# States of the retention layers from token-major keys, values projected once and spread by ScalarE

## The chip, the cores and the metric

One core of one Trainium2 chip runs the whole program. The metric is the device time of one execution in microseconds (us); the median of the runs counts. Engines: PE is TensorE, DVE VectorE, ACT ScalarE, POOL GpSimd, SP SyncE.

## What is computed

Four blocks run one after the other on 2048 tokens of width 128: a selective scan, a soft decision tree, four retention layers and a choice among eight experts, each with norms and residuals. The change touches the retention layers. Cut to that:

```python
Q, K, V = (x @ Wq), (x @ Wk), (x @ Wv)           # 8 heads of 16
Q, K = _rotate(Q, cos, sin), _rotate(K, cos, -sin)
att = jnp.einsum('bnhd,bmhd->bhnm', Q, K) * Dm    # decay gamma^(n-m), n >= m
Y = jnp.einsum('bhnm,bmhd->bnhd', att, V)
Y = normalise(Y) * gn_s + gn_b                     # over the 16 of a head
Yr = (swish(x @ Wg) * Y) @ Wo + X                  # x = layer_norm(X)
X = gelu(layer_norm(Yr) @ W1) @ W2 + Yr
```

## The kernel before

Everything lies in SBUF, in fp32. The tokens are four groups of 512 (two sequences of 256, four tiles of 128). A sequence is cut into chunks of 64. Attention inside a chunk is worked out directly (**scores**, masked by DVE); what earlier chunks contribute goes through a state, keys transposed times values for a chunk (**states**), of which DVE keeps the blocks of one head (its mask), and which **mix** multiplies with the queries. Decay is folded into the tables with which keys and queries are turned.

A layer is a list of steps. SCHEDULE gives each a time in units of one group's turn; the steps of the four groups are sorted by it into one order, LAYER, and every engine goes through this order and issues its part of each step. OPENING is the same list for the first layer, sorted together with the steps of the tree; ENDING that of the last layer, with the steps of the experts (d_turn, logits, oh_turn, hidden, expert). So a turn of the steady part holds each step once, for different groups. An engine waits where a semaphore isn't there yet, and what stands behind waits too.

The steps of a group that the text speaks of, in the order of its way: stats1, norm1 (DVE, with the rstd by POOL, L521 and L523), **turn1** (PE transposes, ACT copies to Ht, L799), **rotate** (PE L1428, keys and queries token-major; DVE L1085 multiplies by cosines into Tc and by sines into Ts), **gate** (PE L1447, ACT's Tanh L814, DVE L1090), **spread** (POOL L628 adds Tc and Ts for keys, then for queries; PE transposes L1435; ACT makes masked copies Ka and Qp), **keys** (PE transposes the masked copies back, L1453; ACT copies to Kt, L833), **values** (PE L1443; ACT L808 writes Va, in which even and odd heads lie on different partitions), **scores** (PE L1464, DVE L1100), **states** (PE L1473, DVE L1110), **mix** (PE L1485 and L1491), **gather** (ACT L836), **heads** and **var** (PE L1499, DVE, POOL's power L636, unit L1131), **out_turn**, **scale** (DVE L1135), **out** (PE L1239, DVE L1138), stats2, norm2 (DVE L919), **ffn_turn**, **ffn_up** (PE L1517, gelu on ACT L853), **ffn_down** (PE L1239, DVE's addition L1146).

PSUM has eight banks of 512 columns. FILLS says which bank a step of PE fills and which event frees it; claim makes PE wait for the event of the bank's last use:

```python
for event, of, at_group, nth in held.get(b, ()):
    pe.wait_ge(*event.at(of, at_group, nth))
held[b] = [(reader, layer, g, k)]
```

Banks 2 and 3 hold scores and, in the ending, hidden; experts use 6 and 7; oh_turn uses 5, d_turn and logits use 1, in both versions.

## Time and profile before

| | |
|---|---|
| median of 3 runs | 774.08 us (773.95 to 774.34) |
| profiled execution | 775.45 us, of which the span from first to last instruction 773.7 |
| PE, DVE, POOL, ACT busy | 649.6, 616.8, 441.6, 426.0 us |
| mean granted clock of PE | 0.95 |

Busy times are sums over the span; the stretches of it have different limits. A PE matmul in fp32 is two records in the trace, a transpose one; their ends are modelled and overlap the next one's start.

### The profile page before, as it was taken

The page shows a single profiled execution, that of the slowest core. Times are in us where ns is not written, and L with a number is a line of the kernel's source. Part 1 is how long each engine was busy: PE and PEld are TensorE (multiplying, and loading weights), DVE is VectorE, ACT ScalarE, POOL GpSimd, SP SyncE. Part 2 cuts the span into 40 slices and gives each one's busy share as a digit, 9 for nine tenths or more (in the row PEclk, how much of TensorE's full clock was granted, in tenths as well). Part 3 has the DMA queues.
Part 4 walks back from the last instruction along what each step waited for, and adds up shares of the span by engine and source line. Part 5 has one row for each costly group of instructions (what it writes and reads, how often), then busy time and mean ns, then how long its engine had stood idle before and what let it go on. Part 6 is the DMA issues. An engine that isn't in the chain of part 4 may idle for free. (4 is left out here: it accounts for less than half of the span.)

```text
span 773.7 us, 13393 instructions
## 1 busy us (share of the span) xinstructions
PE 649.6 (84%) x4919; PEld 449.8 (58%) x4928; DVE 616.8 (80%) x1519; ACT 426.0 (55%) x745; POOL 441.6 (57%) x411
## 2 busy tenths in 40 slices
PE   3997798898988853547889999999999999889994
PEld 1435444444444342545767777777777777657673
DVE  6479798998989777474778888888888888778886
ACT  1896785886767405445545555555555555354551
POOL 6113588786877947564565555556666666452212
PEclk9997799999999996796999999999999999999998
DMA  9003033233233300000000000000000000000000
GB/s 321 13 5 54 28 98 92 82 99 92 77 89 86 75 2 0 0 1 0 2 2 22 2 6 16 21 2 5 15 1 22 3 18 1 2 0 1 1 27 29
DMA packets 17297, 27.37 MB, mean 35 GB/s; under 512 B 2320, under 2 KB 7056, under 8 KB 16976
## 3 DMA queue, kind: packets, MB, share of 16 engines
q1 hardware_dynamic: 17232, 26.51, 12.1%
q8 instruction: 40, 0.66, 0.3%
q14 instruction: 25, 0.20, 0.1%
HBM read 25.32 MB, written 1.18 MB: 34 GB/s over the span
## 5 line engine op out<-in xcount | busy, mean ns | idle before, releaser
L584 POOL TENSOR_TENSOR arena<-arena 128x1024 f32<-128x1024 f32 x64 | 150.1, 2363 | 52.3 <-PE psum L1340 26.8
L1010 DVE TENSOR_TENSOR_SCAN arena<-arena,psum 128x1024 f32<-128x1024 f32 x64 | 141.8, 2269 | 3.3 <-issue 2.0
L1340 PE MATMUL psum<-arena,Cs 128*128 128x512 f32 x256 | 121.9, 599 | 1.2 <-POOL arena L584 1.2
L721 ACT ACTIVATE arena<-arena 128x510 f32<-128x510 f32 x128 | 84.9, 711 | 51.8 <-DVE arena L1010 49.8
L521 POOL TENSOR_TENSOR ve<-mv,eps 128x4 f32<-128x4 f32 x52 | 15.9, 305 | 166.4 <-DVE mv L908 166.4
L636 POOL TENSOR_TENSOR arena<-arena,mhalf 128x32 f32<-128x32 f32 x16 | 86.8, 5428 | 4.5 <-DVE arena L1126 4.5
L1232 PE MATMUL psum<-Cs,arena 128*128 128x128 f32 x240 | 40.2, 292 | 43.0 <-ACT arena L764 25.9
L1340 PEld LDWEIGHTS psum<-arena,Cs 128*128 128x128 f32 x256 | 45.2, 191 | 46.4 <-issue 35.0
L1232 PEld LDWEIGHTS psum<-Cs,arena 128*128 128x128 f32 x240 | 27.8, 147 | 57.9 <-ACT arena L764 27.1
L628 POOL TENSOR_TENSOR arena<-arena 128x256 f32<-128x256 f32 x64 | 57.8, 935 | 2.4 <-DVE arena L1085 2.4
L1239 PE MATMUL psum<-Wl,arena 128*128 128x128 f32 x384 | 51.3, 285 | 5.9 <-DVE arena L1135 5.4
L523 POOL TENSOR_TENSOR rs<-ve,mhalf 128x4 f32<-128x4 f32 x52 | 53.4, 1027 | 4.1
L1323 PE MATMUL psum<-Cs,arena 128*128 128x128 f32 x256 | 35.2, 284 | 23.9 <-ACT arena L743 20.7
L1323 PEld LDWEIGHTS psum<-Cs,arena 128*128 128x128 f32 x256 | 30.2, 146 | 42.2 <-issue 37.6
L743 ACT ACTIVATE arena<-arena 128x256 f32<-128x256 f32 x128 | 54.2, 495 | 0.0
L1239 PEld LDWEIGHTS psum<-Wl,arena 128*128 128x128 f32 x384 | 46.9, 197 | 9.4 <-DVE arena L1135 8.8
L1239 PEld LDWEIGHTS psum<-Wd,arena 128*128 128x128 f32 (+1 forms) x320 | 39.5, 191 | 16.1 <-issue 7.0
L904 DVE BATCH_NORM_STATS2 st<-arena 128x6 f32<-128x128 f32 x208 | 45.2, 280 | 3.9 <-ACT arena L764 2.6
L919 DVE TENSOR_SCALAR arena<-arena,mv,rs 128x128 f32<-128x128 f32 x160 | 44.6, 343 | 3.7 <-POOL rs L523 3.7
L1100 DVE TENSOR_TENSOR arena<-psum,Cs 128x512 f32<-128x512 f32 x64 | 41.0, 683 | 6.5 <-PE psum L1464 6.5
L1239 PE MATMUL psum<-Wd,arena 128*128 128x128 f32 (+2 forms) x320 | 41.8, 276 | 2.8 <-DVE arena L1209 1.4
L1215 DVE SCALAR_TENSOR_TENSOR arena<-psum,arena 128x128 f32<-128x128 f32 x128 | 35.9, 344 | 8.9 <-PE psum L1239 7.5
(175 smaller groups left out, 1396.6 us busy)
## 6 DMA issues: line engine op xcount, KB each, us to landing
arena<-c_rows_by_state SPq DMA_DIRECT2D x32, 512.0 KB, 4.7
Wl<-wl SPq DMA_DIRECT2D x4, 384.0 KB, 3.1
Wd<-wd SPq DMA_DIRECT2D x1, 1100.0 KB, 10.8
X<-x SPq DMA_DIRECT2D x4, 256.0 KB, 6.9
Sel<-sel SPq DMA_DIRECT2D x1, 1024.0 KB, 8.9
Wl<-wl SPq DMA_DIRECT2D x4, 256.0 KB, 2.7
out<-X SPq DMA_DIRECT2D x4, 256.0 KB, 2.3
Cs<-const SPq DMA_DIRECT2D x1, 614.0 KB, 9.6
```

Of the source, the lines that this page charges most:

```text
L523: pool.tensor_tensor(rs[:, g * GT:(g + 1) * GT], ve[:, g * GT:(g + 1) * GT], mhalf[:, 0:GT], ALU.pow).then_inc(rstd_ready, 1)
L584: pool.tensor_tensor(Hc[:, h], Hs[:, r, h], Crows[:, r], ALU.mult).then_inc(hc_ready, 1)
L628: ins = pool.tensor_tensor(to[:, :, :, e], to[:, :, :, e], other[:, :, :, 1 - e], ALU.add)
L636: pool.tensor_tensor(gst[:, cols], gst[:, cols], mhalf[:], ALU.pow).then_inc(rstd_ready, 1)
L721: ins = act.activation(Da[:, h, group(e)].rearrange(seq, s=S)[:, :, 1:], Dt[:, h, group(g)].rearrange(seq, s=S)[:, :, 1:], ACT.Exp, scale= ...
L743: ins = act.activation(Wslot[n % 2][:, part, k, :], Flip[g % 2][:, k * 256:(k + 1) * 256], ACT.Identity, scale=Bt_rows[:, column:column + 1])
L904: own.put(dve.bn_stats(st3[:, t, :], src3[:, t, :]))
L1010: dve.tensor_tensor_scan(Hs[:, turn % 2, h], Da[:, h], rows_of(turn, h), 0.0, ALU.mult, ALU.add).then_inc(scanned, 1)
L1232: ins = pe.transpose(dst[:, tile(k)], src3[:, g * GT + k, :], ident)
L1239: ins = pe.matmul(dst[:, k * width:(k + 1) * width], r[:, tile(k)], w, start=i == 0, stop=i == len(rows) - 1)
L1323: ins = pe.transpose(rows[:, tile(e * GT + k)], Wslot[slot % 2][:, e, k, tile(h)], ident)
L1340: ins = pe.matmul(bank[h], ident, Hc[:, h, group(e)], start=False, stop=False, skip_group_check=True)
```

## The change

Keys are no longer transposed back. States multiplies the token-major turned keys in Tc, 64 tokens of a tile at a time, with plain values Vt in the same tokens; even chunks lie in rows 0 to 63, odd ones in rows 64 to 127, and the two kinds fill two banks (even chunks of both sequences in bank 5, 512 columns, odd ones in bank 7, 256), so that DVE's two masks have these widths. Values is four matmuls of 128 columns, token-major; ACT copies them whole to Vt and then in four quarters to Va, between partitions where needed. Several steps move to other banks. The times of SCHEDULE change, by which gate comes ahead of mix on PE and ahead of gather on ACT, in the opening rx_stats of groups 2 and 3 ahead of the states masks of groups 0 and 1 on DVE, and in the ending x_stats of group 0 ahead of the masks of group 3, and stats2 of group 3 ahead of group 0's last expert sum; else the order on DVE and POOL is the old one.

```diff
-    (1.142, "spread", 1), (1.309, "keys", 0), (1.296, "scores", 0), (1.515, "values", 0), (1.012, "gate", 0),
-    (1.516, "scores", 1), (1.562, "states", 0), (1.957, "mix", 0), (2.010, "gather", 0), (2.068, "heads", 0),
+    (1.138, "spread", 1), (1.299, "scores", 0), (1.511, "values", 0), (0.964, "gate", 0), (1.514, "scores", 1),
+    (1.737, "states", 0), (1.966, "mix", 0), (2.039, "gather", 0), (2.077, "heads", 0), (2.291, "square", 0),
...
-        Kt = take(4 * (SEQ_CHUNKS - 1) * P).rearrange("p (b n) -> p b n", b=4)
+        Vt = take(2 * GT * P).rearrange("p (t n) -> p t n", n=P)
...
-            "rotate": ((4, rotated, 2), (1, rotated, 4)), "spread": ((5, k_spread, 1), (4, q_spread, 1)),
-            "values": ((1, v_ready, 1),), "gate": ((1, sg_ready, 1),),
-            "keys": ((7, k_tokens, 1), (5, k_tokens, 2)), "states": ((5, states, 1), (7, states, 2)),
-            "mix": ((6, yt_rows, 1),), "out": ((4, r_mid, 1),), "ffn_up": ((4, gelu_ready, 1), (7, gelu_ready, 2)), "ffn_down": ((7, r_newer, 1),)}
+            "rotate": ((4, rotated, 2), (1, rotated, 4)), "spread": ((5, k_spread, 1), (1, q_spread, 1)),
+            "values": ((4, v_ready, 1),), "gate": ((7, sg_ready, 1),),
+            "states": ((5, states, 1), (7, states, 2)),
+            "mix": ((6, yt_rows, 1),), "out": ((5, r_mid, 1),), "ffn_up": ((1, gelu_ready, 1), (4, gelu_ready, 2)), "ffn_down": ((4, r_newer, 1),)}
...
                         act.wait_ge(*v_done.at(layer, g))
                         act.wait_ge(*added.at(layer, g - 2))
-                        for a in range(PARITY):
-                            half_rows = slice(CHUNK * a, CHUNK * a + CHUNK)
-                            dst = Va[half_rows, chunks, :].rearrange("p c (j w) -> p (c j) w", j=PAIR)[:, :, DH * a:DH * a + DH]
-                            ins = act.copy(dst, bank[FILLS[what][0][0]][half_rows, :].rearrange("p (c i) -> p c i", i=DH))
-                            if a == 0:
-                                own.put(ins)
+                        tiles = slice(g % 2 * GT, (g % 2 + 1) * GT)
+                        rows = bank[FILLS[what][0][0]]
+                        own.put(act.copy(Vt[:, tiles, :].rearrange("p t n -> p (t n)"), rows))
+                        for e in range(2):
+                            from_rows = rows[CHUNK * e:CHUNK * e + CHUNK, :].rearrange("p (t j a i) -> p t j a i", t=GT, j=PAIR, a=PARITY)
+                            for a in range(PARITY):
+                                to_rows = Va[CHUNK * a:CHUNK * a + CHUNK, chunks, :].rearrange(
+                                    "p (t e) (j a i) -> p t e j a i", e=2, j=PAIR, a=PARITY)
+                                ins = act.copy(to_rows[:, :, e, :, a, :], from_rows[:, :, :, a, :])
+                                if e * PARITY + a < 3:
+                                    own.put(ins)
                         ins.then_inc(v_ready.sem, 1)
...
                             ins = act.copy(Qr[:, half], rows)
                         ins.then_inc(done.sem, 1)
-                    if what == "keys":
-                        for b in range(2):
-                            act.wait_ge(*k_turned.at(layer, g, b + 1))
-                            act.copy(Kt[:, g % 2 * 2 + b, :], bank[FILLS[what][b][0]][:, 0:(SEQ_CHUNKS - 1) * P]).then_inc(k_tokens.sem, 1)
                     if what == "gather":
...
 
                         dve.wait_ge(*kq_turned.at(layer, g - 2))
+                        dve.wait_ge(*states.at(layer, g - 2))
                         for b in range(2):
...
                             if b == 0:
                                 dve.wait_ge(*added.at(layer, g - 2))
-                            width = (SEQ_CHUNKS - 1) * P
-                            own_block = Cs[:, CS["same_head"]].unsqueeze(1).broadcast_to((P, SEQ_CHUNKS - 1, P))
-                            dve.tensor_tensor(States[:, g % 2 * 2 + b, :].rearrange("p (c f) -> p c f", f=P),
-                                              bank[FILLS[what][b][0]][:, 0:width].rearrange("p (c f) -> p c f", f=P),
-                                              own_block, ALU.mult).then_inc(states.sem, 1)
+                            chunks = slice(b, SEQ_CHUNKS - 1, 2)
+                            count = (2, 1)[b]
+                            own_block = Cs[:, CS["same_head"]].unsqueeze(1).unsqueeze(1).broadcast_to((P, 2, count, P))
+                            dve.tensor_tensor(
+                                States[:, g % 2 * 2:g % 2 * 2 + 2, :].rearrange("p s (c f) -> p s c f", f=P)[:, :, chunks, :],
+                                bank[FILLS[what][b][0]][:, 0:2 * count * P].rearrange("p (s c f) -> p s c f", s=2, f=P),
+                                own_block, ALU.mult).then_inc(states.sem, 1)
                     if what == "heads":
...
 
                         dst = claim(what, 0, layer, g)
-                        for c in range(CHUNKS):
-                            for a in range(PARITY):
-                                cols = slice(g * GC + c * CHUNK, g * GC + (c + 1) * CHUNK)
-                                ins = pe.matmul(dst[a * CHUNK:(a + 1) * CHUNK, c * CHUNK:(c + 1) * CHUNK], Ht[:, cols],
-                                                Wl[:, WL["v"]][:, a * (D // 2):(a + 1) * (D // 2)], start=True, stop=True)
+                        in_order = Wl[:, WL["v"]].rearrange("p (a j i) -> p j a i", a=PARITY, j=PAIR)
+                        for t in range(GT):
+                            ins = pe.matmul(dst[:, tile(t)].rearrange("p (j a i) -> p j a i", j=PAIR, a=PARITY),
+                                            Ht[:, group(g)][:, tile(t)], in_order, start=True, stop=True)
                         ins.then_inc(v_done.sem, 1)
                     if what == "gate":
                         pe.matmul(claim(what, 0, layer, g), Wl[:, WL["g"]], Ht[:, group(g)], start=True, stop=True).then_inc(g_done.sem, 1)
-                    if what == "keys":
-                        pe.wait_ge(*k_spread.at(layer, g))
-                        for b in range(2):
-                            dst = claim(what, b, layer, g)
-                            for c in range(SEQ_CHUNKS - 1):
-                                ins = pe.transpose(dst[:, tile(c)], Ka[:, chunk0 + b * SEQ_CHUNKS + c, :], ident)
-                            ins.then_inc(k_turned.sem, 1)
                     if what == "scores":
 
                         if part == 0:
+                            pe.wait_ge(*k_spread.at(layer, g))
                             pe.wait_ge(*q_spread.at(layer, g))
...
                     if what == "states":
                         pe.wait_ge(*v_ready.at(layer, g))
+                        pe.wait_ge(*summed.at(layer, g, 1))
+                        dsts = [claim(what, a, layer, g) for a in range(2)]
                         for b in range(2):
-                            pe.wait_ge(*k_tokens.at(layer, g, b + 1))
-                            dst = claim(what, b, layer, g)
-                            for c in range(SEQ_CHUNKS - 1):
-                                ins = pe.matmul(dst[:, tile(c)], Kt[:, seq0 + b, tile(c)], Va[:, chunk0 + b * SEQ_CHUNKS + c, :],
-                                                start=True, stop=True)
-                            ins.then_inc(state_done.sem, 1)
+                            for c, a, at in sorted(((0, 0, 2 * b), (1, 1, b), (2, 0, 2 * b + 1)), key=lambda x: b * x[1]):
+                                rows = slice(CHUNK * a, CHUNK * (a + 1))
+                                t = g % 2 * GT + 2 * b + c // 2
+                                ins = pe.matmul(dsts[a][:, tile(at)], Tc[rows, t, 0, :], Vt[rows, t, :], start=True, stop=True)
+                                if b == 1 and c > 0:
+                                    ins.then_inc(state_done.sem, 1)
                     if what == "mix":
 
 
                         rows_y = claim(what, 0, layer, g)
                         for b in range(2):
                             y = rows_y[:, b * S:(b + 1) * S]
-                            pe.wait_ge(*states.at(layer, g, b + 1))
+                            if b == 0:
+                                pe.wait_ge(*states.at(layer, g))
                             for c in range(SEQ_CHUNKS - 1):
```

Three places of PE's order follow; names in brackets are the semaphores that a row waits for. First the steady part, from keys to turn1. Before, with L1453 keys, L1239 out, L1443 values, L1464 scores and L1232 turn1:

```order
L1453 MATMUL psum<-Cs,arena 128x128 [waits r_new,k_spread]
L1453 MATMUL psum<-Cs,arena 128x128 x2
L1453 MATMUL psum<-Cs,arena 128x128 [waits k_spread]
L1453 MATMUL psum<-Cs,arena 128x128 x2
L1239 MATMUL psum<-Wl,arena 128x128 [waits q_spread,out_in,gy_rows]
L1239 MATMUL psum<-Wl,arena 128x128 x3
L1443 MATMUL psum<-Wl,arena 64x64 [waits sg_ready]
L1443 MATMUL psum<-Wl,arena 64x64 x15
L1464 MATMUL psum<-arena 128x128 [waits masked]
L1464 MATMUL psum<-arena 128x128 x7
L1232 MATMUL psum<-Cs,arena 128x128 [waits gy_affine,c_normed]
L1232 MATMUL psum<-Cs,arena 128x128 x3
```

After, from scores on, with L1242 out, L1445 values, L1460 scores, L1235 turn1 and L1471 states:

```order
L1460 MATMUL psum<-arena 128x128 [waits masked,q_spread,k_spread]
L1460 MATMUL psum<-arena 128x128 x7
L1242 MATMUL psum<-Wl,arena 128x128 [waits k_spread,gy_rows]
L1242 MATMUL psum<-Wl,arena 128x128 x3
L1445 MATMUL psum<-Wl,arena 128x128 [waits r_new]
L1445 MATMUL psum<-Wl,arena 128x128 x3
L1460 MATMUL psum<-arena 128x128 [waits masked]
L1460 MATMUL psum<-arena 128x128 x7
L1235 MATMUL psum<-Cs,arena 128x128 [waits gy_affine,c_normed]
L1235 MATMUL psum<-Cs,arena 128x128 x3
L1471 MATMUL psum<-arena 128x128 [waits r_mid,sg_ready,summed,v_ready]
L1471 MATMUL psum<-arena 128x128 x5
```

Keys are gone, out follows scores directly, and states waits for the copies of the values (v_ready), for out's reader (r_mid) and gate's (sg_ready) instead of k_tokens.

Second, from mix to ffn_up. Before, with L1485 and L1491 mix, L1447 gate, L1517 ffn_up:

```order
L1485 MATMUL psum<-arena 128x192 [waits states,yt_rows]
L1485 MATMUL psum<-arena 128x128
L1485 MATMUL psum<-arena 128x64
L1491 MATMUL psum<-arena 32x64 [waits masked]
L1491 MATMUL psum<-arena 32x64 x15
L1485 MATMUL psum<-arena 128x192 [waits states]
L1485 MATMUL psum<-arena 128x128
L1485 MATMUL psum<-arena 128x64
L1491 MATMUL psum<-arena 32x64 [waits masked]
L1491 MATMUL psum<-arena 32x64 x15
L1447 MATMUL psum<-arena,Wl 128x512 [waits rotated]
L1517 MATMUL psum<-arena,Wl 128x512 [waits rotated,f_rows]
```

After, with L1235 ffn_turn, L1449 gate, L1484 and L1490 mix:

```order
L1235 MATMUL psum<-Cs,arena 128x128 [waits hn_rows,f_normed]
L1235 MATMUL psum<-Cs,arena 128x128 x3
L1449 MATMUL psum<-arena,Wl 128x512 [waits states]
L1484 MATMUL psum<-arena 128x192 [waits states,yt_rows]
L1484 MATMUL psum<-arena 128x128
L1484 MATMUL psum<-arena 128x64
L1490 MATMUL psum<-arena 32x64 [waits masked]
```

Gate has moved ahead of mix and waits for the masks of states, whose input was in its bank; before it waited for rotate's reader.

Third, the ending, from the first hidden step to the first expert of group 0. Before, with L1565 hidden, L1555 oh_turn, the first L1239 out and the second an expert:

```order
L1565 MATMUL psum<-arena,Wd 128x512 [waits d_rows,masked]
L1555 MATMUL psum<-Cs,arena 8x128 [waits states,chosen]
L1555 MATMUL psum<-Cs,arena 8x128 x3
L1239 MATMUL psum<-Wl,arena 128x128 [waits gelu_ready,gy_rows]
L1239 MATMUL psum<-Wl,arena 128x128 x3
L1565 MATMUL psum<-arena,Wd 128x512 [waits d_rows,masked]
L1239 MATMUL psum<-Wd,arena 128x128 [waits oh_rows,yt_rows]
```

After, with L1564 hidden, L1554 oh_turn, L1242 out and expert:

```order
L1564 MATMUL psum<-arena,Wd 128x512 [waits d_rows,masked]
L1554 MATMUL psum<-Cs,arena 8x128 [waits states,chosen]
L1554 MATMUL psum<-Cs,arena 8x128 x3
L1242 MATMUL psum<-Wl,arena 128x128 [waits oh_rows,gy_rows]
L1242 MATMUL psum<-Wl,arena 128x128 x3
L1564 MATMUL psum<-arena,Wd 128x512 [waits d_rows,masked]
L1242 MATMUL psum<-Wd,arena 128x128 [waits oh_rows,yt_rows]
```

The order is the same; out waits for oh_rows (ACT's copy of oh_turn's result) where it waited for gelu_ready.

## Rows read from the trace of the kernel before

**Rows 1.** Three windows; the first line names the columns.

```profile
core 0: us, PE busy (x) PEld busy (x) DVE busy (x) ACT busy (x) POOL busy (x), PEclk, DMA share, GB/s
420.00:640.00 220.00, 211.54 (x2471) 172.49 (x2468) 184.18 (x515) 112.90 (x189) 130.32 (x99) 1.00 0.04 12
390.90:394.30 3.40, 1.85 (x11) 1.02 (x10) 0.56 (x2) 2.61 (x6) 3.32 (x6) 1.00 0.00 0
672.10:675.50 3.40, 3.40 (x18) 3.40 (x18) 2.54 (x12) 0.61 (x2) 0.00 (x0) 0.50 0.00 0
```

**Rows 2.** Timeline of DVE, one turn: start, length, instruction, idle before.

```profile
515.01 0.69 DVE L1146 TENSOR_TENSOR arena<-psum,arena 128x512 f32<-128x512 f32 x1 [1.43 <-PE psum L1239]
...
524.75 1.02 DVE L1110 TENSOR_TENSOR arena<-psum,Cs 128x384 f32<-128x384 f32 x2
...
534.80 0.69 DVE L1146 TENSOR_TENSOR arena<-psum,arena 128x512 f32<-128x512 f32 x1 [1.44 <-PE psum L1239]
```

**Rows 3.** Timeline of POOL in the same turn.

```profile
521.91 0.20 POOL L521 TENSOR_TENSOR ve<-mv,eps 128x4 f32<-128x4 f32 x1 [3.15 <-DVE mv L908]
...
523.17 5.43 POOL L636 TENSOR_TENSOR arena<-arena,mhalf 128x32 f32<-128x32 f32 x1
```

**Rows 4.** Timeline of PE in the same turn.

```profile
515.34 1.16 PE L1464 MATMUL psum<-arena 64*128 64x128 f32 x16
516.43 0.88 PE L1453 MATMUL psum<-Cs,arena 128*128 128x128 f32 x6
517.65 1.16 PE L1239 MATMUL psum<-Wl,arena 128*128 128x128 f32 x8 [0.35 <-DVE arena L1135]
518.74 1.15 PE L1443 MATMUL psum<-Wl,arena 128*64 128x64 f32 x32
...
521.41 1.50 PE L1473 MATMUL psum<-arena 128*128 128x128 f32 x12
522.75 1.89 PE L1428 MATMUL psum<-Wl,arena 128*128 128x256 f32 x8
524.89 0.66 PE L1232 MATMUL psum<-Cs,arena 128*128 128x128 f32 x4 [0.25 <-DVE arena L919]
525.45 0.95 PE L1485 MATMUL psum<-arena 128*128 128x192 f32 x6
...
532.32 0.66 PE L1435 MATMUL psum<-Cs,arena 128*128 128x128 f32 x4 [0.19 <-POOL arena L628]
532.81 1.95 PE L1239 MATMUL psum<-Wl,arena 128*128 128x128 f32 x16
```

**Rows 5.** Groups of ACT instructions by form, 420 to 640 us.

```profile
L808 ACT COPY arena<-psum 64x512 f32<-64x512 f32 x24 | 13.9, 581 | 25.5 <-issue 25.3
...
L833 ACT COPY arena<-psum 128x384 f32<-128x384 f32 x22 | 9.5, 482 | 3.0 <-PE psum L1453 3.0
```

**Rows 6.** Timeline of all engines, while the layers start.

```profile
362.07 1.54 PE L1453 MATMUL psum<-Cs,arena 128*128 128x128 f32 x6
...
373.09 3.25 POOL L628 TENSOR_TENSOR arena<-arena 128x256 f32<-128x256 f32 x4
...
393.36 0.59 ACT L814 ACTIVATE arena<-psum 128x512 f32<-128x512 f32 x1
...
393.51 0.66 PE L1499 MATMUL psum<-Cs,arena 128*128 128x128 f32 x4 [1.55 <-ACT arena L836]
```

**Rows 7.** Timeline of all engines, while the experts run.

```profile
669.90 0.66 PE L1232 MATMUL psum<-Cs,arena 128*128 128x128 f32 x4 [1.04 <-DVE arena L919]
...
678.55 1.16 PE L1239 MATMUL psum<-Wl,arena 128*128 128x128 f32 x8 [0.95 <-DVE arena L1135]
...
679.54 0.56 ACT L881 COPY arena<-psum 8x512 f32<-8x512 f32 x1
...
710.40 1.11 DVE L919 TENSOR_SCALAR arena<-arena,mv,rs 128x128 f32<-128x128 f32 x4 [1.41 <-POOL rs L523]
...
720.04 1.12 PE L1517 MATMUL psum<-arena,Wl 128*128 128x512 f32 x2 [1.57 <-DVE arena L1215]
```

More of the change, by code:

```diff
@@ L173 @@
 SCHEDULE = (
-    (0.192, "stats1", 0), (0.399, "norm1", 0), (0.533, "turn1", 0), (0.816, "rotate", 0), (1.087, "spread", 0),
-    (1.142, "spread", 1), (1.309, "keys", 0), (1.296, "scores", 0), (1.515, "values", 0), (1.012, "gate", 0),
-    (1.516, "scores", 1), (1.562, "states", 0), (1.957, "mix", 0), (2.010, "gather", 0), (2.068, "heads", 0),
-    (2.295, "square", 0), (2.509, "var", 0), (2.835, "unit", 0), (3.161, "out_turn", 0), (3.276, "scale", 0),
-    (3.447, "out", 0), (3.507, "stats2", 0), (3.532, "norm2", 0), (3.912, "ffn_turn", 0), (4.053, "ffn_up", 0),
-    (4.152, "ffn_down", 0),)
+    (0.218, "stats1", 0), (0.411, "norm1", 0), (0.529, "turn1", 0), (0.751, "rotate", 0), (1.130, "spread", 0),
+    (1.138, "spread", 1), (1.299, "scores", 0), (1.511, "values", 0), (0.964, "gate", 0), (1.514, "scores", 1),
+    (1.737, "states", 0), (1.966, "mix", 0), (2.039, "gather", 0), (2.077, "heads", 0), (2.291, "square", 0),
+    (2.505, "var", 0), (2.842, "unit", 0), (3.157, "out_turn", 0), (3.272, "scale", 0), (3.443, "out", 0),
+    (3.481, "stats2", 0), (3.528, "norm2", 0), (3.908, "ffn_turn", 0), (4.053, "ffn_up", 0),
+    (4.144, "ffn_down", 0),)
 def layer_order():
@@ L403, in four_blocks @@
         kq_turned = per_group("kq_turned", 2, 1)
-        k_turned, k_tokens = per_group("k_turned", 2), per_group("k_tokens", 2, 1)
         scores, masked = per_group("scores", 4), per_group("masked", 4, 1)
@@ L412, in four_blocks @@
         w1_done, gelu_ready, w2_done = per_group("w1_done", 2), per_group("gelu_ready", 2, 1), per_group("w2_done")
-        primed = (hn_rows, kq_turned, v_ready, sg_ready, k_tokens, masked, states, added, yt_rows, centred,
+        primed = (hn_rows, kq_turned, v_ready, sg_ready, masked, states, added, yt_rows, centred,
                   gy_affine, r_mid, f_rows, gelu_ready)
```

## The prediction

> **What bounds the kernel now.** I read the share of busy time by windows first. Over the layers (420 to 640 us) PE is busy 211.54 of 220 us at the full clock, DVE 184.18, POOL 130.32, ACT 112.90 [rows 1]. That names PE, and the change takes work from PE. But a busy PE is made of matmuls whose modelled ends overlap, so I went on to the timelines of the engines over one turn (one group of 512 tokens), to see who is waiting for whom.
>
> DVE's first instruction of a turn is the addition of ffn_down. It starts at 515.01, after waiting 1.43 for PE, and again at 534.80 [rows 2]: the period is 19.79. From 515.01 DVE runs without a wait through stats1, scale, the masks of scores, norm1, out and stats2. POOL, idle until then, starts at 521.91 [rows 3], 6.90 after the addition began. It works out the rstd of stats2, then from 523.17 the power of the heads' variances (5.43), then the two additions of spread. PE's second spread (of the queries) waits for them and starts at 532.32 [rows 4], 10.41 after POOL began. Behind it stands ffn_down, 532.81 to 534.76, and the next addition follows at 534.80: 2.48. So 6.90 + 10.41 + 2.48 = 19.79: the period is a ring DVE, POOL, PE (spread and ffn_down), DVE. Keys, values and states are not on it.
>
> A second path is nearly as long: DVE to norm2, for which ffn_turn on PE waits 0.25 at 524.89, then PE without a pause through mix, gate, ffn_up and heads to the second spread, where it waits 0.19 for POOL [rows 4]. The row counts that wait from the modelled end of the first spread, so I take 0.2 to 0.35 as what this path has to spare.
>
> **The layers, part by part** (about 12 periods of 19.79 between the opening and the ending).
>
> *Keys go* (6 transposes and 2 copies a group). PE is relieved of the 0.88 at 516.43. But out, next in its row, already waits 0.35 for scale on DVE at 517.65 [rows 4], and scale follows stats1 in DVE's part of the ring. Out starts no earlier, and PE waits from 516.43 to 517.65, 1.2. Worth 0.
>
> *Values* become 4 matmuls of 128 columns, in the form of out: 8 records in 1.16 where 32 take 1.15 [rows 4]. Worth 0 on PE. On ACT two copies of 64x512 become one of 128x512 and four of 64x256. No row has the last form. From 581 ns for 512 columns and 482 for 384 [rows 5] a column costs 0.77 ns, which leaves 0.38 us for 256 columns; bounds are 0.30 (only the columns and a little) and 0.58 (as long as 512). The five take about 2.2 us instead of 1.2, and end near 522.1 where states could start at 521.4. So states waits about 0.7.
>
> *States*: 12 records with 64 rows, in alternating halves of the array for the most part. The nearest rows are scores, of that form, 16 in 1.16, and states now, 12 in 1.50 [rows 4]: between 0.87 and 1.50, I take 1.1. Started at 522.1 it ends at 523.2, rotate (1.7 from start to start) at 524.9 instead of 524.5. Then ffn_turn starts at 525.0, not 524.89.
>
> *Gate ahead of mix, in bank 7.* Mix needed only the first of DVE's two masks of states (1.02 for both, from 524.75 [rows 2]) and started at 525.45 [rows 4]. Gate takes the bank of the second mask's input, so it must wait for both, until 525.85. The masks have the same columns as before (512 + 256 for 384 + 384). This covers the late ffn_turn, and makes the second path 0.4 longer, against 0.2 to 0.35 to spare. I take +0.05 a period, with bounds 0 and +0.2: +0.6 in all, 0 to +2.5. A gain is excluded, since no instruction on the ring gets shorter. The other new bank waits (spread of the queries behind the first gelu, ffn_up behind rotate) end over 0.3 before their instruction's turn in this timeline.
>
> **The opening.** Before the ring closes, the chain runs through keys: at 362.07 the first group's keys take PE 1.54, at half clock [rows 6], and values, scores and DVE's masks wait in line behind them, with POOL's spread at 373.09 at the chain's end. DVE also takes rx_stats ahead of the masks of states, on which POOL's work before that spread hangs. Some 1.5 us come off, and most stays until the second group's heads. There ACT now does gate's Tanh (0.59 at 393.36) ahead of the copy of y, for which PE's heads wait 1.55 at 393.51 [rows 6]; that gives back about 0.4. Net -1.2, with bounds 0 (a cold clock eats it) and -2.2.
>
> **The ending.** Four things. (1) x_stats of group 0 now precedes the masks of states, mix of group 3 is late by that step, but PE then idles 1.04 at 669.90 [rows 7]: +0.3. (2) Out moves to bank 5, which oh_turn has filled just ahead of it. Out of group 2 started at 678.55; now it waits for ACT's copy at 679.54, which lasts until 680.10 [rows 7]: +1.55, and with (1) +1.85. (3) stats2 of group 3 moves ahead of an expert's sum on DVE; norm2's wait of 1.41 for POOL at 710.40 [rows 7] goes: -1.4. (4) ffn_up leaves bank 7, so the wait of 1.57 for DVE at 720.04 [rows 7] goes; but d_turn now shares bank 1 with ffn_up and waits for the first gelu, so I keep -0.65. That makes -0.2. If ffn_down of group 1 no longer falls into the stretch 672.1 to 675.5, which ran at 1.2 GHz [rows 1] after PE had idled, the copy comes 1.65 earlier and the sum is -1.85. PE idles less ahead of it in the change, but no row tells when the clock falls, so I take the middle, -1.0.
>
> **Sum.** -1.2 + 0.6 - 1.0 = -1.6. The profiled execution took 775.45 (a span of 773.7), 1.4 above the median of the runs, 774.08. The terms are differences, so I set them against the median: 772.5.
>
> **Rivals.**
> *PE is the bound after all* (211.54 of 220 busy): then keys (0.88) and states (0.4) come off each period, 12 x 1.3 = 15 us, 759. Against it: the three parts of the ring add up to the period to the last hundredth. Chance 0.07.
>
> *Slower, by ACT's copies of the values.* If the four small copies take 0.58 each, like those with twice the columns [rows 5], states starts at 522.9, rotate ends at 525.7, ffn_turn starts at 525.8 and gate at 526.3, 0.45 beyond the time at which the masks let it go. The second path then is the longer one: +0.5 x 12 = +6, less 2.2 from the ends, 778. It decides from about 0.48 a copy. For it: the 25.5 us in which ACT stood ready before L808 [rows 5] were a cover that is now used up; against it, the two rows fix the slope. Chance 0.20.
> The Trainium skill's page "ScalarE: Activation LUTs" (section "Rules for kernel authors") budgets about 0.3 us for an ACTIVATE and 0.83 ns for an element. By that, an estimate from the page, the five take 2.8 us, and the rival comes true in part, at some 776. The rows here fix 0.19 + 0.77 ns, so I keep my number.
>
> *The clock falls in the layers*, with PE idle 1.2 before out and 0.7 before states. The page "Perfetto Trace Analysis" of the Trainium skill (section "Matmul Optimizations") says that the engine scales its power with use and wants matmuls back to back. In this trace the clock stayed at full speed in the stretch 390.9 to 394.3, in which PE was busy for 1.85 of 3.40 us [rows 1]. At half clock ffn_down and the spread (2.4 on the ring) would double: +29, 803. Chance 0.03.
>
> *The gains of both ends are lost* (the cold stretch stays, the opening's chain is bound by POOL): 774.0 to 775.5. Chance 0.15.
>
> **How the numbers follow.** My own case has 0.55 and reaches from 769.8 (-2.2 and -1.9, layers 0) to 774.5. The range takes in the slower rival and leaves out PE as the bound and the cold clock: 769 to 778.5. A measurement here tells a change from none at about 0.2% (1.5 us): faster is below 772.5. My case lies about half below that; its bounds reach farther down than up, so I count 0.34 of its 0.55 there, and PE as the bound adds 0.07: 0.41. The same: the other 0.21 of my case and the lost gains, 0.15: 0.36. Slower: the copies, 0.20, and the clock, 0.03: 0.23.
>
> **What would show it.** Right: the period between ffn_down's additions on DVE stays at 19.79 to 19.85, POOL's power still follows stats2's rstd at once, PE shows a wait of about 1.0 to 1.2 for scale before out and one of 0.5 to 0.9 for ACT before states, its busy share falls with no gain in time; gate starts at the end of the second mask; the layers start 1 us earlier; out of group 2 waits for the copy of oh_turn; no wait for an expert's sum inside ffn_up. Wrong: a period shorter by 0.3 or more (PE was the bound), or longer with a copy over 0.48.

## The result, and the profile after

The changed kernel took 777.52 us (median of 5 runs, 776.41 to 778.31) where the kernel before took 773.95 beside it (773.52 to 774.34): 1.0045 times, 95% interval 1.0030 to 1.0059. It is slower, by about 3.5 us. Measured again on another chip it was 1.0027 times before (1.0012 to 1.0043). The profiled execution has a span of 774.6 us for 773.7.

One turn in the layers, on DVE (start, length, instruction, idle before), of the changed kernel:

```profile
515.58 0.69 DVE L1149 TENSOR_TENSOR arena<-psum,arena 128x512 f32<-128x512 f32 x1 [1.03 <-PE psum L1242]
...
525.31 1.02 DVE L1112 TENSOR_TENSOR arena<-psum,Cs 128x512 f32<-128x512 f32 x2
...
535.36 0.69 DVE L1149 TENSOR_TENSOR arena<-psum,arena 128x512 f32<-128x512 f32 x1 [1.03 <-PE psum L1242]
```

The same turn on PE, below it ACT's copies of the values, and the form of the four small ones, 420 to 640 us (busy, mean ns, idle before):

```profile
516.35 1.16 PE L1460 MATMUL psum<-arena 64*128 64x128 f32 x16 [0.37 <-issue]
518.22 1.16 PE L1242 MATMUL psum<-Wl,arena 128*128 128x128 f32 x8 [0.72 <-DVE arena L1138]
...
522.42 1.16 PE L1471 MATMUL psum<-arena 64*128 64x128 f32 x12 [0.47 <-ACT arena L812]
...
526.38 1.13 PE L1449 MATMUL psum<-arena,Wl 128*128 128x512 f32 x2 [0.28 <-DVE arena L1112]
...
532.50 1.04 PE L1438 MATMUL psum<-Cs,arena 128*128 128x128 f32 x8
533.37 1.95 PE L1242 MATMUL psum<-Wl,arena 128*128 128x128 f32 x16
```

```profile
520.36 0.59 ACT L806 COPY arena<-psum 128x512 f32<-128x512 f32 x1 [2.91 <-issue]
520.84 1.54 ACT L812 COPY arena<-psum 64x256 f32<-64x256 f32 x4
```

```profile
L812 ACT COPY arena<-psum 64x256 f32<-64x256 f32 x46 | 16.8, 366 | 0.8
```

The turn is as forecast: 19.78 from addition to addition (19.79 in [rows 2]). PE waits 0.37 and 0.72 for what the keys covered, 0.47 for ACT before states (L1471), 0.28 for the second mask before gate (L1449). Nothing of it reaches the additions; the spreads of keys and queries now run as one, without a wait for POOL.

Most of the loss stands at the two ends. Windows of the changed kernel, then of the one before (us, busy of each engine, PEclk, DMA share, GB/s):

```profile
420.00:640.00 220.00, 199.71 (x2119) 160.43 (x2117) 183.20 (x513) 110.63 (x201) 130.67 (x100) 1.00 0.04 11
380.00:402.00 22.00, 19.08 (x177) 16.05 (x176) 16.06 (x47) 9.41 (x19) 11.35 (x11) 0.77 0.01 1
660.00:676.00 16.00, 11.87 (x120) 9.46 (x121) 9.54 (x38) 5.19 (x9) 9.05 (x6) 0.79 0.01 2
```

```profile
380.00:402.00 22.00, 18.69 (x252) 15.81 (x252) 16.61 (x48) 10.84 (x21) 11.37 (x11) 0.95 0.01 2
660.00:676.00 16.00, 12.63 (x131) 10.51 (x131) 10.79 (x44) 4.66 (x7) 8.54 (x6) 0.89 0.00 1
```

PE has 11.83 us less to do in the layers, for nothing. In the opening the granted clock was 0.77 for 0.95, in the ending 0.79 for 0.89: at half (1.2 GHz) between 393.7 and 400.6, where before had full speed, and between 663.4 and 670.2, where before had 672.1 to 675.5.

I cut the span at marks that every trace has: the first matmul of the first rotate; DVE's 1st and 13th addition of ffn_down; the end. Opening, twelve periods and ending lie between them. Of before (two traces), the change (three) and the kernels of the experiments, in us; the last column sets each kernel's time against before on the same chip:

| kernel | opening | 12 periods | ending | times before (95%) |
|---|---|---|---|---|
| before | 66.38, 66.36 | 237.47, 237.35 | 120.13, 120.07 | |
| the change | 67.43, 67.70, 67.42 | 237.41, 238.20, 238.05 | 120.55, 120.65, 120.26 | 1.0027 (1.0012 to 1.0043) |
| new forms, old table | 66.43 | 238.15 | 120.14 | 1.0008 (0.9992 to 1.0025) |
| change, old order | 66.95 | 238.10 | 120.06 | 1.0031 (1.0015 to 1.0048) |
| change, gate behind mix everywhere | 66.00 | 238.12 | 122.31 | 1.0001 (0.9986 to 1.0016) |
| change, states first on DVE | 68.01 | 237.97 | 120.85 | 1.0032 (1.0017 to 1.0046) |
| change, oh_turn in bank 1 | 67.92 | 237.65 | 119.53 | 1.0017 (1.0001 to 1.0033) |
| change, states after one copy | 68.16 | 238.16 | 120.65 | 1.0032 (1.0017 to 1.0047) |
| change, gate behind mix in the opening | 66.14 | 238.12 | 120.80 | 1.0012 (0.9998 to 1.0027) |
| change, matmuls in every wait | 68.63 | 238.70 | 119.52 | 1.0038 (1.0020 to 1.0055) |
| change, matmuls in long waits | 66.62 | 237.52 | 119.56 | 1.0000 (0.9985 to 1.0015) |
| four edits | 65.75 | 237.53 | 118.36 | 0.9963 (0.9949 to 0.9978) |
| five edits | 65.57 | 237.37 | 116.72 | 0.9946 (0.9932 to 0.9960) |

On average of its traces the change lost 1.15 in the opening, 0.48 in the layers and 0.39 in the ending, 2.0 of the 2.3 to 3.5 that the medians show. The rest is not settled: single executions of one kernel differ by more (before: 772.1 to 779.3 in 35 runs on one chip).

### The profile page after: what moved, and what is told of

Same layout as the page of the kernel before. It is cut to its first block and busy times, and to the rows that moved or that the text cites. A ratio compares the mean times of both kernels' runs of the same rounds, so it can differ in the third digit from the quotient of the medians.

```text
span 774.6 us, 12433 instructions
## 1 busy us (share of the span) xinstructions
PE 635.2 (82%) x4439; PEld 436.3 (56%) x4448; DVE 615.1 (79%) x1519; ACT 423.1 (55%) x761; POOL 441.1 (57%) x410
## 5 line engine op out<-in xcount | busy, mean ns | idle before, releaser
L1343 PE MATMUL psum<-arena,Cs 128*128 128x512 f32 x256 | 123.6, 606 | 1.2 <-POOL arena L583 1.2
L1235 PE MATMUL psum<-Cs,arena 128*128 128x128 f32 x240 | 41.7, 301 | 39.7 <-ACT arena L763 25.2
L1242 PE MATMUL psum<-Wl,arena 128*128 128x128 f32 x384 | 50.5, 282 | 12.7 <-DVE arena L1138 9.3
L1235 PEld LDWEIGHTS psum<-Cs,arena 128*128 128x128 f32 x240 | 28.7, 151 | 53.9 <-ACT arena L763 26.4
L1242 PEld LDWEIGHTS psum<-Wl,arena 128*128 128x128 f32 x384 | 45.9, 193 | 15.9 <-DVE arena L1138 14.7
L1326 PE MATMUL psum<-Cs,arena 128*128 128x128 f32 x256 | 35.4, 285 | 23.4 <-ACT arena L742 20.8
L1460 PE MATMUL psum<-arena 64*128 64x128 f32 x512 | 40.6, 302 | 9.8 <-issue 9.8
L1242 PEld LDWEIGHTS psum<-Wd,arena 128*128 128x128 f32 (+1 forms) x320 | 39.6, 191 | 14.4 <-issue 7.7
L826 ACT ACTIVATE arena<-psum,Cs 128x512 f32<-128x512 f32 x64 | 38.8, 688 | 9.3 <-PE psum L1438 9.3
## 6 DMA issues: line engine op xcount, KB each, us to landing
Wd<-wd SPq DMA_DIRECT2D x1, 1100.0 KB, 10.8
```

The source lines that it names most:

```text
L1235: ins = pe.transpose(dst[:, tile(k)], src3[:, g * GT + k, :], ident)
L1242: ins = pe.matmul(dst[:, k * width:(k + 1) * width], r[:, tile(k)], w, start=i == 0, stop=i == len(rows) - 1)
L1326: ins = pe.transpose(rows[:, tile(e * GT + k)], Wslot[slot % 2][:, e, k, tile(h)], ident)
L1343: ins = pe.matmul(bank[h], ident, Hc[:, h, group(e)], start=False, stop=False, skip_group_check=True)
```

## The experiments

**Forms or table?** The change has new forms of values and states, and a new table of positions and banks. First the new forms with the table of before (keys left out of it). Here and below a diff shows only the entries that matter of each line:

```diff
-(1.737, "states", 0), (0.964, "gate", 0)
+(1.562, "states", 0), (1.012, "gate", 0)
...
-"gate": ((7, sg_ready, 1),), "out": ((5, r_mid, 1),)
+"gate": ((1, sg_ready, 1),), "out": ((4, r_mid, 1),)
...
```

> The changed values, states and copies, without the keys, but in the order of the kernel before and with its banks. Theory A (order and banks: the 3.5 us were lost at the two ends, where DVE now takes rx_stats and x_stats ahead of the masks of states and out waits for the copy of oh_turn): 771.5 to 774.0, no slower than before. Theory B (the new forms: five copies on ACT, less work on PE, and a clock that falls more often for it, whatever the order): 776 to 778, and the stretches at half clock in the opening and around 665 us are there again.

775.51 us, 1.0008 times before: in the time the forms neither cost nor gain, though each period is 0.06 longer. There is no half clock between 385 and 402, though PE has the smaller work. So in the opening less work alone does not bring the clock down, against theory B, and the new table does the harm. In the ending theory B is not refuted: the new forms alone have half clock from 664.2 to 667.6, where before has it from 672.1, and so has, starting between 662.3 and 665.3, every kernel with the new forms whose waits there are not filled. Here it cost nothing: 22.38 from the 13th addition to the 14th, 22.37 before. The other half, old forms in the new order:

```diff
-(1.562, "states", 0), (1.012, "gate", 0), (1.309, "keys", 0)
+(1.737, "states", 0), (0.964, "gate", 0), (1.305, "keys", 0)
...
```

> The kernel before, keys included, with the changed order of the steps and its own banks. Theory A: the late masks of states come back at both ends (1.7 us each in DVE's row, of which about 1 stays in the opening and 1 to 1.6 in the ending), 775 to 777. Theory B: 773.5 to 774.5, as before.

831.56 us, 1.0719 times before, which neither theory expected. PE's timeline, one turn:

```profile
554.45 1.74 PE L1447 MATMUL psum<-arena,Wl 128*128 128x512 f32 x2 [2.67 <-DVE arena L1085]
```

Gate, now ahead of mix, still fills bank 1, where rotate's rows stand until DVE (L1085) is through: 2.67 us of waiting in each turn, the clock at half in a stretch of every turn, and a period of 23.76. So order and banks can't be tried apart this way; gate's move needs its bank 7.

**The parts of the table, one by one.**

```diff
-"oh_turn": ((5, oh_rows, 1),)
+"oh_turn": ((1, oh_rows, 1),)
```

> The changed kernel with oh_turn in bank 1 instead of 5, so that out no longer waits for ACT's copy of oh_turn. Theory A: PE's wait of 2.64 us before out of group 2 falls to about 1 (then it waits for scale on DVE), that of 0.76 before out of group 3 goes, 1.0 to 2.0 us less than the change, 775.5 to 776.5. Theory B: less than 0.5 us, since other work fills the gap.

777.31 us, 1.0017. The wait before out of group 2 goes from 2.64 (for ACT's L881) to this, of PE's timeline:

```profile
681.33 1.16 PE L1242 MATMUL psum<-Wl,arena 128*128 128x128 f32 x8 [1.83 <-DVE arena L1138]
```

The two stretches of the ending that hold out of groups 2 and 3 become 24.15 to 23.38 and 25.08 to 24.39 long (from one addition of ffn_down to the next): 1.46 together, about as much as I had priced for one (+1.55). In the median of the runs this is within the noise.

```diff
-(1.737, "states", 0)
+(1.580, "states", 0)
```

> The changed kernel with states at 1.580 in the table instead of 1.737: PE's order stays, DVE takes the masks of states ahead of rx_stats in the opening and ahead of x_stats in the ending again. Theory A: heads of the first group and mix of group 3 start 0.8 and 1.1 to 1.6 us earlier, the time is 1.5 to 3 us below the change, 774.5 to 776. Theory B: unchanged, 777 to 778, or moved only by where stretches at half clock happen to lie.

778.93 us, 1.0032: no gain. Mix of group 3 starts 1.2 earlier after the 13th addition (10.8 for 12.0), but the stretch at half clock lies there as in the change and another came at 681. Theory A, order and banks as waits alone, fails here.

```diff
-(0.964, "gate", 0)
+(1.045, "gate", 0)
```

> The changed kernel with gate at 1.045 in the table instead of 0.964, so behind mix on PE and behind the copy of y on ACT, as in the order of before; everything else stays as changed. Theory C (gate's Tanh ahead of the copy of y makes PE wait 1.83 us before heads of the second group instead of 1.55, and with the wait before scores of the third the clock falls at 393.7): heads of the second group is 0.4 us earlier, no half clock between 390 and 402, the layers start 1.5 us earlier than in the change. Theory D (the stretches at half clock come from the new banks or the order of DVE and not from gate): a stretch at half clock between 390 and 402 is there again, and the time is that of the change within 0.7 us.

775.57 us, 1.0001: the opening is 1.4 to 1.7 shorter and has no half clock after 381, as theory C has it. The period rises to 19.84, and the ending to 122.31, with half clock from 664 to 671 and from 681 to 685. The whole order of before, with the new banks:

```diff
-(1.737, "states", 0), (0.964, "gate", 0)
+(1.562, "states", 0), (1.012, "gate", 0)
...
```

> The changed kernel, new banks included, in the order of the kernel before without its keys. With the order of before and its banks the time was that of before; with the order of before and its steps alone undone the question is what the banks add. Theory A (the order is the cause): no half clock between 390 and 402, at most one short stretch near 665, 774.5 to 776.5 on a chip where before takes 776. Theory D (the banks are): out of groups 2 and 3 waits for the copy of oh_turn, 1.0 to 2.5 us are lost in the ending alone, 777 to 779 there.

778.10 us, 1.0031. Its trace has 66.95 and 120.06 at the ends, which is theory A's side, its time is theory D's: inconclusive. Its period, 19.84, says something else: with gate behind mix the new forms cost 0.06 a turn (three kernels agree), and gate's move gives this back.

> The changed kernel once more, beside the others on their chip. If the 3.5 us are the change's own: 1.003 to 1.006 times before here too, with half clock between 390 and 402 and between 663 and 671. If they were chance, in how the chip's clock fell in those five runs: 0.999 to 1.002.

777.77 us, 1.0027: the loss is the change's own. Here a weight load of the next layer (384 KB, between values of group 3 and rotate of group 0) came late:

```profile
505.37 1.97 PE L1431 MATMUL psum<-Wl,arena 128*128 128x256 f32 x8 [1.37 <-issue]
```

```profile
Wl<-wl SPq DMA_DIRECT2D x1, 384.0 KB, 4.5
```

In the first trace that load took 3.0 us. The late rotate made one period 20.49. In other traces of kernels that keep gate ahead of mix in the layers, a rotate up to 0.7 late cost nothing, 0.85 late 0.1, 1.07 late 0.34. The third trace of the change lost 0.70 at the same place, two traces of before nothing.

**Gate in the opening alone.** In the opening, gate's two matmuls now stand ahead of mix, whose output ACT copies for heads. Of the change, all engines, while the layers start:

```profile
370.11 1.13 PE L1449 MATMUL psum<-arena,Wl 128*128 128x512 f32 x2
...
370.97 1.65 ACT L763 ACTIVATE arena<-X,shift,rs 128x128 f32<-128x128 f32 x4 [1.40 <-POOL shift L534]
371.07 0.88 PE L1484 MATMUL psum<-arena 128*128 128x192 f32 x6
...
374.10 0.58 ACT L836 COPY arena<-psum 128x512 f32<-128x512 f32 x1 [1.00 <-PE psum L1490]
...
374.74 0.66 PE L1498 MATMUL psum<-Cs,arena 128*128 128x128 f32 x4 [0.71 <-ACT arena L836]
...
393.01 0.66 PE L1498 MATMUL psum<-Cs,arena 128*128 128x128 f32 x4 [1.83 <-ACT arena L836]
```

Gate takes 0.96 (370.11 to 371.07), and the copy of y waits 1.00 for mix. In the kernel before, and with the new forms in the old table, the copy waited for nothing on PE: it stood behind ACT's normalisation (L764, L763), which waits for POOL. Those rows of before, then of the new forms with the old table:

```profile
371.94 1.65 ACT L764 ACTIVATE arena<-X,shift,rs 128x128 f32<-128x128 f32 x4 [2.61 <-POOL shift L535]
...
373.50 0.56 ACT L836 COPY arena<-psum 128x512 f32<-128x512 f32 x1
```

```profile
370.88 1.65 ACT L763 ACTIVATE arena<-X,shift,rs 128x128 f32<-128x128 f32 x4 [2.88 <-POOL shift L534]
...
372.44 0.56 ACT L836 COPY arena<-psum 128x512 f32<-128x512 f32 x1
...
373.05 0.66 PE L1498 MATMUL psum<-Cs,arena 128*128 128x128 f32 x4 [0.45 <-ACT arena L836]
```

```diff
-for t, what, k in SCHEDULE if g + t < G])]
+for t, what, k in ((1.045 if what == "gate" and g < G - 1 else t, what, k)
+                   for t, what, k in SCHEDULE) if g + t < G])]
```

> The changed kernel with gate behind mix (and behind the copy of y) in the opening alone, for groups 0 to 2; the order of the layers and the ending stays as changed. Theory C2 (in the opening gate's two matmuls stand 0.9 to 1.1 us ahead of mix on the chain that ends in heads, and in the layers they cost nothing): rotate.0 to the first ffn_down addition falls from 67.4 to 67.7 to 66.0, the period stays at 19.79, half clock between 393 and 402 goes; 1.4 to 1.7 us below the change, 1.0005 to 1.0015 times before. Theory H (gate behind mix helped in the run that had it everywhere through the ending or by chance): as the change, 1.002 to 1.004.

776.50 us, 1.0012; opening 66.14, period back at 19.79 but for one late weight load. Half clock came once more, at 396.1 to 399.5, against theory C2. The gain all lies ahead of it: heads of the second group start 42.8 after the first rotate, 43.8 to 44.5 in the change, and from there to heads of the third group it takes 20.0, as in the change (19.9 to 20.4). So gate's place alone costs 1.0 to 1.7 there by this trace, 0.4 to 1.1 by that of the kernel with gate behind mix everywhere (43.4).

**The small copies.**

```diff
-pe.wait_ge(*v_ready.at(layer, g))    # states
+pe.wait_ge(*v_plain.at(layer, g))    # after the whole copy; mix waits for v_ready
```

> The changed kernel, but states waits for the whole copy of the values alone (a semaphore of its own); mix waits for the four small copies. Nothing else moves. Theory F (the small copies ate what the keys gave back in the opening: states stands 0.5 to 1.5 us behind them there): rotate.0 to heads of the first group is 0.5 to 1.0 us shorter, the first ffn_down addition 0.5 to 1.5 us earlier, the period stays 19.79, the ending is the same; 1.000 to 1.002 times before. Theory G (the ring and the copy of y set the opening, states has nothing to give): the time of the change, 1.002 to 1.004 times before.

778.32 us, 1.0032: nothing gained (theory G); 0.6 of it is a late weight load. The wait only moves on to rotate, whose input ACT writes behind the small copies, as the groups of PE from 420 to 640 us show:

```profile
L1431 PE MATMUL psum<-Wl,arena 128*128 128x256 f32 x88 | 21.8, 391 | 4.6 <-ACT arena L798 2.8 <-issue 1.8
```

**The clock.** Transposes of the identity that compute nothing, in places where PE waits (the edits in short):

```diff
+for k in range(n): pe.transpose(<bank filled next>, ident, ident)
+ n = 12 ahead of heads, 12 ahead of the first scores, 8 ahead of mix
```

> The changed kernel with extra transposes of the identity on PE in the opening and the ending only: 12 ahead of the wait of heads, 12 ahead of the wait of the first scores, 8 ahead of the wait of mix, into the bank that the step then overwrites. It computes nothing with them. Theory C (PE's idle time at the two ends costs the clock, and the clock the time): the stretches at half clock after 350 go but for one or two, the layers start 1 to 2 us earlier, the time falls by 2 to 4 us below the change. Theory E (half clock there is a follower: the chain waits for ACT, DVE and POOL, and PE's speed matters little): the clock rises and the time stays within 0.7 us, or gets longer by the added matmuls.

778.20 us, 1.0038: the half clock after 360 is gone, the time is not. But they also stand where PE has no time to give: heads in the opening's first group is later, and the last of the twelve periods, where the ending's first heads has them, is 21.09. That spoils the test; so only in waits that are long enough:

```diff
+ 12 ahead of heads 1; 12 and 6 ahead of the first scores 1 and 2 (opening)
+ 14 ahead of ffn_turn 1; 8 ahead of mix 3 (ending)
```

> The changed kernel with transposes of the identity that fit into waits of PE: 12 ahead of heads of the second group, 12 and 6 ahead of the first scores of the second and third, 14 ahead of ffn_turn of group 1 and 8 ahead of mix of group 3 in the ending. They compute nothing. Theory C (idle PE, then half clock, then time): no half clock between 390 and 402 nor between 663 and 671, each worth 1.0 to 1.5 us, 2 to 3 us below the change, 0.999 to 1.000 times before. Theory E (half clock there costs little beside the waits for ACT and DVE): within 0.7 us of the change, 1.002 to 1.004.

775.56 us, 1.0000 times before, for 1.0027 of the change. Windows:

```profile
380.00:402.00 22.00, 17.92 (x205) 14.75 (x204) 16.40 (x56) 11.30 (x24) 11.89 (x11) 1.00 0.01 1
660.00:676.00 16.00, 14.36 (x155) 11.10 (x154) 10.99 (x42) 6.47 (x9) 7.60 (x4) 1.00 0.01 2
```

Full clock in both places. The opening is 0.8 to 1.1 shorter, and from the 13th addition to the 14th it is 22.06 for 23.7 to 24.1. But half clock came back in the ending from 677.5 to 680.9, at out of group 2, whose wait nothing fills:

```profile
678.03 2.05 PE L1242 MATMUL psum<-Wl,arena 128*128 128x128 f32 x8 [2.64 <-ACT arena L881]
```

The next stretch, to the 15th addition, is 25.07 for 24.15, so half of that gain goes again. Theory C holds: PE's waits there cost the clock, and the clock costs time, though its work is on no chain in the layers.

**Better than both.** Gate behind mix in the opening, oh_turn in bank 1, x_stats at 4.740 (behind the masks of states on DVE), states after one copy; then the transposes of the ending besides:

> The changed kernel with four edits: gate behind mix in the opening, oh_turn in bank 1, x_stats at 4.740 so that DVE masks the states of group 3 first, and states waiting for one copy. If the losses are where the stages say (opening +1.0 to +1.3, ending +0.4, with 1.0 more to gain there since out's wait was 2.64): opening 65.5 to 66.0, layers 237.4 to 238.2, ending 118 to 119, together 3 to 4 us below the change and 0.998 to 0.9995 times before. If the ends are set by half clock stretches that come back elsewhere: 1.000 to 1.003.

772.38 us, 0.9963. What each of the four gives here was not told apart.

> The kernel with the four edits, and 14 transposes of the identity ahead of ffn_turn of group 1 and 8 ahead of mix of group 3 in the ending, where PE waits; they compute nothing. If half clock around 665 costs the ending beside the order of DVE's steps: no stretch there, the part of the ending between the 13th and the 14th ffn_down addition falls from 23.2 to about 21.5 to 22.1, 1 to 1.5 us below the four edits, 0.994 to 0.9965 times before. If the order of DVE's steps had been all of it, or the stretch comes back at 677 and takes the same: 0.9955 to 0.9975.

770.99 us, 0.9946. Full clock in the ending:

```profile
660.00:676.00 16.00, 13.49 (x148) 10.49 (x146) 11.41 (x42) 6.32 (x9) 8.15 (x6) 1.00 0.01 2
```

The stretch to the 14th addition is 21.62 (23.24 with four edits). Both kernels come out by stage as expected; the time with four edits is below the 0.998 to 0.9995 that I expected. In the opening half clock is still there with five edits, from 397.8 to 401.2.

> The kernel before, a second trace, so that the losses by stage don't rest on one. If the stages are its own: 66.0 to 66.8 from the first rotate to the first ffn_down addition, 237.4 to 237.6 for twelve periods, 120.0 to 120.4 for the ending, with no half clock between 390 and 402. If they are chance: over 67 in the opening, or a period with a late weight load of over 20 us.

> The changed kernel, a third trace beside that of before on the same chip. If the losses by stage are its own: 67.3 to 68.2 in the opening with half clock between 390 and 402, 237.4 to 238.2 for twelve periods, 120.4 to 120.8 in the ending with half clock around 665. If they are chance, the opening or the ending comes out as that of before.

774.40 and 775.67 us, one run each. The stages repeat (table), to 0.1 us for before; the change has half clock from 392.6 to 399.5 and from 662.3 to 669.1 again.

## Why the prediction was wrong

The forecast was 772.5; the direction was wrong, because of both ends.

**The layers were right**, and the +0.05 a period too cautious: 19.78. The ring is unbroken, keys are worth 0, a small copy takes 0.366 us (0.38 taken), states 1.16 (1.1), its wait 0.47 (0.7). The slower rival needed 0.48 a copy and did not come true; that the time fell near its 778 is chance. The five copies took 2.0 us (520.36 to 522.38). By the budget of the Trainium skill's page "ScalarE: Activation LUTs" (section "Rules for kernel authors") they would have taken 2.8, an estimate from the page. PE as the bound is excluded by 11.83 us less work at the same period. What I missed: the load of the next layer's weights, between values and rotate, which came late in two traces of three and cost 0.7; whether the change makes it later is open (at that place it took 3.0, 4.5 and 4.5 in the change, 3.0 and 3.1 in before, 3.0 to 3.7 in the three kernels with the new forms and gate behind mix everywhere). The lower end of my own case was added wrongly, 769.8 for 770.0; nothing hangs on it.

**The opening, -1.2, failed**: measured +1.05 to +1.32. Two steps. First, "some 1.5 us come off, and most stays until the second group's heads": with the new forms in the old table values do start 1.2 earlier after rotate (12.6 for 13.8), but 0.17 is left at heads, because its input waits behind ACT's normalisation, and that for POOL. The chain was POOL and ACT, not the keys. Second, "that gives back about 0.4" counted gate's Tanh on ACT in front of the copy and left out gate's two matmuls in front of mix on PE (0.96), which I had costed in the layers alone: heads of the first group start 25.1 to 25.5 after the first rotate, 24.4 in before. By heads of the second group two of the three traces have made this up (43.8, as in before; 44.5 in the other), but the forecast gain is gone. Then the clock fell from 393.7: from heads of the second group to that of the third it took 19.9 to 20.4 in the change, 19.2 to 19.4 in the five kernels with the new forms that had full clock there (20.3 in a sixth, with transposes in the way). Matmuls in PE's waits keep it up; which wait decides is not shown. PE waited 1.83 before heads there for 1.55 [rows 6], but 1.85 with gate behind mix everywhere, where the clock stayed.

**The ending, -1.0, failed by its clock**: measured +0.39 on average. Out's wait (2.64 for 0.95, [rows 7]) was right in kind: the forecast was +1.55 for out of group 2, and undoing it gave 0.77 there and 0.69 at out of group 3. The waits at 710.40 and 720.04 went about as forecast (the first is 0.43 now, the second is gone): from the 15th addition to the 16th 25.08 for 26.22, out of group 3's new wait included. What failed is "PE idles less ahead of it in the change" and, built on it, "so I take the middle" on the clock. These rows show the place, of the change and then of before:

```profile
660.92 1.16 PE L1471 MATMUL psum<-arena 64*128 64x128 f32 x12 [1.06 <-ACT arena L812]
663.88 1.12 PE L1235 MATMUL psum<-Cs,arena 128*128 128x128 f32 x4 [1.81 <-DVE arena L919]
666.07 1.73 PE L1484 MATMUL psum<-arena 128*128 128x192 f32 x6 [1.08 <-DVE arena L1112]
...
673.30 0.60 PE L1498 MATMUL psum<-Cs,arena 128*128 128x128 f32 x4
...
681.52 1.13 PE L1242 MATMUL psum<-Wl,arena 128*128 128x128 f32 x8 [2.64 <-ACT arena L881]
```

```profile
659.75 1.60 PE L1473 MATMUL psum<-arena 128*128 128x128 f32 x12 [0.24 <-ACT arena L808]
663.35 0.66 PE L1232 MATMUL psum<-Cs,arena 128*128 128x128 f32 x4 [2.00 <-DVE arena L919]
663.91 0.95 PE L1485 MATMUL psum<-arena 128*128 128x192 f32 x6
...
670.39 0.60 PE L1499 MATMUL psum<-Cs,arena 128*128 128x128 f32 x4
...
675.90 0.69 DVE L1146 TENSOR_TENSOR arena<-psum,arena 128x512 f32<-128x512 f32 x1 [0.65 <-PE psum L1239]
```

PE idles more, not less: it waits 1.06 for ACT's copies before states and 1.08 for the late masks before mix, where before it waited 0.24 and not at all; the wait of 1.81 for norm2 is the old one of 2.00. The half clock did not go away but came earlier, onto mix: +1.3 to +1.7 to the 14th addition. With the waits filled this stretch is 22.06, no longer than before (22.37), though mix starts as late as in the change (11.9 after the 13th addition, 12.0 in the change, 10.4 in before): the loss against before is the clock's. The +0.3 for x_stats was near: heads of group 3 start 17.28 after the 13th addition with the waits filled, 16.85 in before, and 19.23 in the change at half clock. The old stretch at half clock, priced at 1.65, had held up DVE's addition by 0.65 only (its wait at 675.90).

**The lost gains** (774.0 to 775.5, "the cold stretch stays, the opening's chain is bound by POOL") named both causes at 0.15, but only as gains that stay away, not as losses.

## What to carry to other kernels

One table that orders several stages must be priced stage by stage: gate's move gave 0.06 a turn in the layers and cost about 1 us at the start, where mix was on the chain. Work taken from an engine that waits is not gained, and its clock may fall where its waits come together; look at the granted clock there, at the ends of the program too. When a step gets another bank, look at who empties that bank, in the ending too.

## What was unexpected of the hardware

Matmuls that compute nothing made this kernel faster: 6 to 14 transposes in each of five of PE's waits kept the granted clock at 2.4 GHz around 393 and 663 us, where it had fallen to 1.2, and the time went from 1.0027 to 1.0000 times before (each against before on its own chip). The Trainium skill's page "Perfetto Trace Analysis" (section "Matmul Optimizations") says that the matmul engine's power follows its use and wants matmuls back to back. These two stretches agree (PEclk 0.77 and 0.79, with the waits filled 1.00); I had weighed the page for the layers alone, where the clock stayed at full speed. Where PE waits 2.67 us in every turn, the clock fell in every turn (old forms in the new order). Which waits bring it down, and which do not, no run here tells. And the same load of 384 KB took 3.0 us in one execution and 4.5 in another, at the same place; why is open.
